# Routed experts on one NeuronCore: gate rows formed on chip instead of gathered, expert rows gathered seven tiles ahead

## What is computed

```
mod = silu(c) @ wmod                      # per batch: sa, ca, ga, sb, cb, gb, 512 each
x   = x + ga * attention(layernorm(x) * (1 + ca) + sa)
h   = layernorm(x) * (1 + cb) + sb
idx = top_k(sigmoid(h @ gate_w.T) + router_bias, 2)          # 2 of 8 experts for each token
w   = chosen scores / their sum
x   = x + gb * (sum over the 2 experts of w * W2[e](silu(h W1[e]) * (h W3[e])) + shared expert(h))
```

## Time and profile before

| | |
|---|---|
| median of 3 runs | 1270.96 us (1268.59 to 1273.08) |
| the profiled execution | 1276.45 us |
| its span, first to last instruction | 1274.7 us |
| PE / DVE / ACT / POOL busy | 95% / 52% / 29% / 43% |
| mean granted clock | 0.987 |
| DMA queues' packet time: q1 (SP's and ACT's among them) / q0 (POOL's) | 40.0% / 26.3% |

### The profile page before, as it was taken

How to read it: one execution, slowest core, us unless ns; L and a number is a source line. 1 busy time by engine, 2 the same in 40 slices (tenths; PEclk the granted TensorE clock), 3 DMA queues, 4 the chain that set the end, 5 groups by cost and what they waited for, 6 DMA issues and landing times.

```text
span 1274.7 us, 25045 instructions
## 1 busy us (share of the span) xinstructions
PE 1209.9 (95%) x9054; PEld 778.4 (61%) x9054; DVE 660.1 (52%) x1357; ACT 372.8 (29%) x802; POOL 545.9 (43%) x479
## 2 busy tenths in 40 slices
PE   7999999999998999999999999899999988999986
PEld 2646666666666666667767767465555555656543
DVE  5557778778765777476765534132223222223312
ACT  4334444444433333333333423011111111111111
POOL 2214556656554444301211102355565555555553
PEclk9999999999999999999999999899999999999988
DMA  7915798998797886453543533679798899898794
GB/s 228 234 44 154 168 220 203 224 228 197 196 197 199 214 221 167 101 131 91 113 129 91 136 80 69 133 153 180 155 177 166 153 164 149 176 179 176 160 159 77
DMA packets 258787, 203.60 MB, mean 160 GB/s; under 512 B 187616, under 2 KB 199904, under 8 KB 258668
## 3 DMA queue, kind: packets, MB, share of 16 engines
q1 hardware_dynamic: 217224, 114.14, 40.0%
q0 software_dynamic: 26192, 64.24, 26.3%
q10 hardware_dynamic: 15256, 23.62, 6.4%
HBM read 104.63 MB, written 53.53 MB: 124 GB/s over the span
## 4 chain that ended last, share of the span: by engine, by line
PE 34%; DMA 30%; issue 14%; POOL 12%; DVE 7%; ACT 2%; SPq 0%; POOLq 0%; ACTq 0%; DVEq 0%
DMA out<-y,slot_row 24%; PE ps_vs L86 3%; PE ps_vs L88 3%; PE ps_vs L87 3%; PE ps_vh L86 2%; POOL h L342 2%; PE ps_vh L88 2%; PE ps_vh L87 2%; PE ps_kh L86 2%; PE ps_kh L88 2%; PE ps_kh L87 2%; POOL xg L350 2%; POOL ol L355 2%; DMA xt<-g 2%; PE ps_qh L86 2%
## 5 line engine op out<-in xcount | busy, mean ns | idle before, releaser
L86 PE MATMUL ps_o<-w_all,xt 128*128 x568 | 181.1, 319 | 31.8 <-DMA xt<-g 31.6
L438 POOL DMA_INDIRECT out<-y,slot_row x71 | 114.4, 1611 | 164.7 <-DMA out<-y,slot_row 122.1
L88 PE MATMUL ps_o<-w_all,xt 128*128 x568 | 180.8, 318 | 0.0
L87 PE MATMUL ps_o<-w_all,xt 128*128 x568 | 180.8, 318 | 0.0
L369 POOL DMA_INDIRECT out<-s_sum,row_no x32 | 53.6, 1675 | 237.6 <-DVE s_sum L622 232.1
L856 DVE SCALAR_TENSOR_TENSOR a<-ps_o,a 128x352 f32<-128x352 f32 x71 | 37.3, 525 | 219.9 <-PE ps_o L88 219.9
L1109 ACT ACTIVATE at<-ps_y 128x384 f16<-128x384 f32 x71 | 34.9, 491 | 264.0 <-PE ps_y L1319 264.0
L868 DVE SCALAR_TENSOR_TENSOR y<-ps_vs,slot_weight,gbr 128x512 f32<-128x512 f32 x71 | 53.3, 751 | 102.5 <-PE ps_vs L88 94.0
L331 POOL TENSOR_TENSOR h<-cen,rows_f 128x512 f32<-128x512 f32 x32 | 40.6, 1270 | 130.0 <-ACT cen L886 113.5
L86 PEld LDWEIGHTS ps_o<-w_all,xt 128*128 128x128 f16 x568 | 56.4, 99 | 64.8 <-issue 37.4
L86 PE MATMUL ps_qh<-ht,wqkv 128*128 128x128 f16 x512 | 87.4, 219 | 1.6 <-DVE wqkv L590 1.6
(11 more groups left out here) (244 smaller groups left out, 3325.4 us busy)
## 6 DMA issues: line engine op xcount, KB each, us to landing
w_stage<-in_w_d ACTq DMA_DIRECT2D x64, 176.0 KB, 2.7
xb<-in_x SPq DMA_DIRECT2D x32, 256.0 KB, 3.3
xr<-in_x SPq DMA_DIRECT2D x32, 256.0 KB, 3.7
out<-x SPq DMA_DIRECT2D x32, 256.0 KB, 3.6
h_d<-hl SPq DMA_DIRECT2D x32, 256.0 KB, 2.5
h2t_d<-h2t SPq DMA_DIRECT2D x32, 256.0 KB, 3.7
s_ht<-h2t_d SPq DMA_DIRECT2D x32, 256.0 KB, 3.6
sstage<-in_sh_flat SPq DMA_DIRECT2D x32, 136.0 KB, 3.2
```

The source lines that it names most:

```text
L86: nc.tensor.matmul(out, lh, rh, start=first, stop=False, skip_group_check=True)
L87: nc.tensor.matmul(out, lh, rl, start=False, stop=False, skip_group_check=True)
L88: return nc.tensor.matmul(out, ll, rh, start=False, stop=last, skip_group_check=True)
L438: pool.indirect_dma_start(m.out, bass.IndirectOffsetOnAxis(ap=m.slot_row[:, t:t + 1], axis=0), m.y[:, t % Y_RING, :], None, compute_op=ALU ...
```

## The change

- `gb_rows_d`, its stores, `slot_batch`, `gbr` and `gather_gate` are gone. `list_tokens` makes instead `batch_weight[b]`, for each slot its weight where its batch is b and 0 elsewhere (one copy and four operations of 128x71 more).
- SP loads the four gate rows, broadcast to 128 partitions, into `gate_rows`, 256 KB each, behind the transposes of tiles 0 to 3.
- Each tile's gate row is a sum of four products: ACT makes the first (`first_gate_row`, an activation with a scale from each partition), DVE adds three (`gate_rows_of`), all 128x512 fp32 in SBUF. `e_out` is now one product of PSUM and this row.
- `G_RING` is 6, so `gather(t + 7)` stands behind `scatter(t)`. The new buffers lie over the shared expert's, so gathers 2 to 6 all wait for `up_done` of the last step, and `e_high(0)` for the shared expert's last add.
- Gathers 0 and 1 now stand ahead of `add_shared(14)`.

```diff
-G_RING, GB_RING, Y_RING = 4, 3, 3
+G_RING, GW_RING, Y_RING = 6, 2, 3
@@ SP
-            for b in range(2):
-                sp.dma_start(rows_of(m.gb_rows_d, b), m.s_gb[:, b, :]).then_inc(m.gb_rows_stored, 16)
...
+    for t in range(4):
+        turn_g(t)
+    sp.wait_ge(m.up_done, EARLY_STEPS)
+    for b in range(B):
+        sp.dma_start(m.gate_rows[:, b, :], m.mod_d[b, 5 * C:6 * C].partition_broadcast(P)).then_inc(m.gates_loaded, 16)
+    for t in range(4, SLOT_TILES):
         turn_g(t)
@@ POOL
-    for q in range(TAIL_STEPS, EARLY_STEPS):
+    for q in range(TAIL_STEPS, EARLY_STEPS - SH_TILES):
         if add_due(q):
             add_shared(q // SH_TILES - 1)
     pool.wait_ge(m.listed, 1)
     pool.wait_ge(m.w_lo, E * WP)
     gather(0)
     gather(1)
-    pool.wait_ge(m.s_t1_done, 3 * BT)
-    pool.wait_ge(m.gb_rows_stored, 16 * B)
-    gather_gate(0)
-    pool.wait_ge(m.at_lo, EARLY_STEPS)
-    gather(2)
-    gather(3)
-    gather_gate(1)
-    gather_gate(2)
-    gather(4)
+    add_shared(CHUNKS - 2)
+    pool.wait_ge(m.up_done, EARLY_STEPS)
+    for t in range(2, G_RING + 1):
+        gather(t)
     add_shared(CHUNKS - 1)
...
     for t in range(SLOT_TILES):
         scatter(t)
         gather(t + G_RING + 1)
-        gather_gate(t + GB_RING)
@@ DVE
+    def gate_rows_of(t, b):
+        v.wait_ge(m.gate_first if b == 1 else m.gate_sum, t + 1 if b == 1 else (B - 1) * t + b - 1)
+        row = m.gate_row[t % GW_RING][:, :]
+        v.scalar_tensor_tensor(out=row, in0=m.gate_rows[:, b, :], scalar=m.batch_weight[:, b, t:t + 1], in1=row,
+                               op0=ALU.mult, op1=ALU.add).then_inc(m.gate_sum, 1)
+
     def e_out(t):
...
-        v.scalar_tensor_tensor(out=m.y[:, t % Y_RING, :], in0=m.ps_ey[:, 0:C], scalar=m.slot_weight[:, t:t + 1], in1=m.gbr[r][:, :],
-                               op0=ALU.mult, op1=ALU.mult).then_inc(m.ey_ready, 1)
+        v.tensor_tensor(m.y[:, t % Y_RING, :], m.ps_ey[:, 0:C], m.gate_row[t % GW_RING][:, :], ALU.mult).then_inc(m.ey_ready, 1)
...
-    for t in range(1, SLOT_TILES):
+    for t in range(1, SLOT_TILES + 1):
         e_low(t - 1)
-        e_multiply(t)
+        gate_rows_of(t - 1, 1)
+        gate_rows_of(t - 1, 2)
+        if t < SLOT_TILES:
+            e_multiply(t)
+        gate_rows_of(t - 1, 3)
         e_out(t - 1)
@@ ACT
+        if t == 0:
+            act.wait_ge(m.s_t1_done, 2 * CHUNKS)          # in e_high
...
+    def first_gate_row(t):
+        at_least(act, m.ey_ready, t - GW_RING + 1)
+        if t == 0:
+            act.wait_ge(m.gates_loaded, 16 * B)
+        act.activation(m.gate_row[t % GW_RING][:, :], m.gate_rows[:, 0, :], ACT.Copy, scale=m.batch_weight[:, 0, t:t + 1]).then_inc(m.gate_first, 1)
+
     e_silu(0)
+    first_gate_row(0)
     for t in range(1, SLOT_TILES):
         e_high(t - 1)
+        first_gate_row(t)
         e_silu(t)
```

More of the change, by code:

```diff
@@ L299, in turn_g @@
     def turn_g(t):
[L300 to L309, removed]
+        if t == 2:
+            sp.wait_ge(m.up_done, EARLY_STEPS - SH_TILES)
+        if t == 4:
+            sp.wait_ge(m.up_done, EARLY_STEPS)
+        sp.wait_ge(m.gathered[t % G_RING], ring_use(t, G_RING))
+        at_least(sp, m.h3_done, t - G_RING + 1)
+        sp.dma_start_transpose(m.xt[t % G_RING][:, :, :], m.g[t % G_RING][:, :]).then_inc(m.xt_loaded[t % G_RING], 16)
+    for t in range(4):
+        turn_g(t)
+    sp.wait_ge(m.up_done, EARLY_STEPS)
+    for b in range(B):
+        sp.dma_start(m.gate_rows[:, b, :], m.mod_d[b, 5 * C:6 * C].partition_broadcast(P)).then_inc(m.gates_loaded, 16)
+    for t in range(4, SLOT_TILES):
         turn_g(t)
@@ L816, in list_tokens @@
         step(v.tensor_copy(m.slot_token[:, :], m.tokenf[:, :]))
-        step(v.tensor_scalar(m.slot_batch[:, :], m.slot_token[:, :], (N // P).bit_length() - 1, None, ALU.logical_shift_right))
+        step(v.tensor_scalar(m.batch_i[:, :], m.slot_token[:, :], N.bit_length() - 1, None, ALU.logical_shift_right))
+        step(v.tensor_copy(m.batchf[:, :], m.batch_i[:, :]))
         step(v.tensor_tensor(m.weightf[:, :], m.listing[:, :, 1], m.listing[:, :, 2], ALU.add))
         step(v.tensor_scalar(m.slot_weight[:, :], m.weightf[:, :], 1.0 / SCALE ** 2, None, ALU.mult))
+        for b in range(B):
+            step(v.scalar_tensor_tensor(out=m.batch_weight[:, b, :], in0=m.batchf[:, :], scalar=float(b), in1=m.slot_weight[:, :],
+                                        op0=ALU.is_equal, op1=ALU.mult))
         step(v.tensor_scalar(m.weightf[:, :], m.weightf[:, :], 0.0, None, ALU.is_le))
@@ L861, in e_low @@
         v.tensor_tensor(m.at[:, t % 2, 1, :, :], m.ps_a[:, :, :], m.at[:, t % 2, 0, :, :], ALU.subtract).then_inc(m.e_at_lo, 1)
+    def gate_rows_of(t, b):
[3 more added lines that the diff above has]
+                               op0=ALU.mult, op1=ALU.add).then_inc(m.gate_sum, 1)
     def e_out(t):
-        r = t % GB_RING
         v.wait_ge(m.ey_done, t + 1)
-        v.wait_ge(m.gbr_loaded[r], ring_use(t, GB_RING))
+        v.wait_ge(m.gate_sum, (B - 1) * (t + 1))
         at_least(v, m.scattered, 16 * (t - Y_RING + 1))
-        v.scalar_tensor_tensor(out=m.y[:, t % Y_RING, :], in0=m.ps_ey[:, 0:C], scalar=m.slot_weight[:, t:t + 1], in1=m.gbr[r][:, :],
-                               op0=ALU.mult, op1=ALU.mult).then_inc(m.ey_ready, 1)
+        v.tensor_tensor(m.y[:, t % Y_RING, :], m.ps_ey[:, 0:C], m.gate_row[t % GW_RING][:, :], ALU.mult).then_inc(m.ey_ready, 1)
     e_multiply(0)
     add(CHUNKS - 1)
-    for t in range(1, SLOT_TILES):
+    for t in range(1, SLOT_TILES + 1):
         e_low(t - 1)
-        e_multiply(t)
+        gate_rows_of(t - 1, 1)
[3 more added lines that the diff above has]
+        gate_rows_of(t - 1, 3)
         e_out(t - 1)
-    e_low(SLOT_TILES - 1)
-    e_out(SLOT_TILES - 1)
 def scalar_program(nc, m, act):
@@ L1366, in place_buffers @@
     END = nc.sbuf_usable_end
-    KEPT = FIRST + 5792
+    KEPT = FIRST + 6400
     SHARED_AT = KEPT + 2 * SH_COLS * 2
@@ L1382, in place_buffers @@
     m.spare_row = sb("spare_row", [P, 1], F32)
-    m.slot_weight = sb("slot_weight", [P, SLOT_TILES], F32)
+    m.batch_weight = sb("batch_weight", [P, B, SLOT_TILES], F32)
     m.eid = sb("eid", [1, SLOT_TILES], I32)
@@ L1492, in place_buffers @@
     m.rowf = sb("rowf", [P, SLOT_TILES], F32)
+    m.slot_weight = sb("slot_weight", [P, SLOT_TILES], F32)
+    m.batch_i = sb("batch_i", [P, SLOT_TILES], I32)
+    m.batchf = sb("batchf", [P, SLOT_TILES], F32)
     sb = region(NAMES_AT + 2 * TILES * E * 4, W_END)
@@ L1495, in place_buffers @@
     m.passed = sb("passed", [1, SLOT_TILES, E], F32)
[L1496 to L1500, removed]
+    GATE_AT, ACT_AT, AT_AT, UP_BYTES = SHARED_AT + 8192, SHARED_AT + 12288, SHARED_AT + 14336, UP_COLS * 2
+    staged, third, second = region(W_STAGE_AT, W_AT), region(SHARED_AT, SHARED_AT + 4096), region(SHARED_AT + 4096, SHARED_AT + 8192)
+    high, low = region(KEPT, KEPT + UP_BYTES), region(KEPT + SH_COLS * 2, KEPT + SH_COLS * 2 + UP_BYTES)
+    m.g = [(staged, staged, second, second, high, high)[j](f"g{j}", [P, 2 * C], F16) for j in range(G_RING)]
+    m.xt = [(staged, staged, third, third, high, high)[j](f"xt{j}", [P, 2 * KC, P], F16) for j in range(G_RING)]
+    m.gate_rows = low("gate_rows", [P, B, C], F32)
+    m.gate_row = [(high, low)[j](f"gate_row{j}", [P, C], F32) for j in range(GW_RING)]
     m.y = region(AT_AT, AT_AT + 6144)("y", [P, Y_RING, C], F32)
@@ L1503, in place_buffers @@
     m.a = sb("a", [P, 2, IT * P], F32)
-    m.at = sb("at", [P, 2, 2, IT, P], F16)
+    m.at = region(GATE_AT, ACT_AT)("at", [P, 2, 2, IT, P], F16)
 def name_semaphores(m, sem):
@@ L1538, in name_semaphores @@
     m.w_loaded, m.w_hi, m.w_lo = ring("w_loaded", W_RING), sem("w_hi"), sem("w_lo")
-    m.gathered, m.xt_loaded, m.gbr_loaded = ring("gathered", G_RING), ring("xt_loaded", G_RING), ring("gbr_loaded", GB_RING)
+    m.gathered, m.xt_loaded = ring("gathered", G_RING), ring("xt_loaded", G_RING)
+    m.gates_loaded, m.gate_first, m.gate_sum = sem("gates_loaded"), sem("gate_first"), sem("gate_sum")
     m.scattered, m.spare_stored = sem("scattered"), sem("spare_stored")
-    m.gb_rows_stored = sem("gb_rows_stored")
     m.h1_done, m.h3_done, m.e_silu, m.e_act = sem("h1_done"), sem("h3_done"), sem("e_silu"), sem("e_act")
@@ L1555, in adaln_block @@
     m.h2_d, m.h2t_d = dram("h2_d", (T, 2 * C), F16), dram("h2t_d", (TILES, P, 2 * C), F16)
-    m.mod_d, m.gab_d, m.gb_rows_d = dram("mod_d", (B, 6 * C), F32), dram("gab_d", (B, C), F32), dram("gb_rows_d", (B * P, C), F32)
+    m.mod_d, m.gab_d = dram("mod_d", (B, 6 * C), F32), dram("gab_d", (B, C), F32)
     with ExitStack() as ctx:
```

8 lines of the change are left out of this document (removed).

## The result

| | before | after |
|---|---|---|
| median (10 runs each, 3 of before from the table above) | 1270.08 us (1261.98 to 1279.01) | 1264.90 us (1260.69 to 1267.02) |
| ratio, 95% interval | | 0.9939 [0.9915, 0.9963] |
| profiled execution / span | 1276.45 / 1274.7 us | 1265.33 / 1263.6 us |
| first and last expert scatter start | 822.6 / 1266.8 | 815.6 / 1255.6 |

1264.9 lies outside the range of 1226 to 1260. The change is faster, but the 24 us of the expert loop didn't come. Of the two profiled spans' difference, 11.1 us, 7.0 come before the first scatter and 4.2 from the loop. These are one execution each, and the one of before lies 6.4 us above its kernel's median. The medians differ by 5.2, less than the start alone brings, so the loop's gain may be nothing.

A forecast was written before the change was run, and what follows sets the result against it. The prediction took the chain of expert scatter landings, 6.35 us a tile, to bound the kernel. From the median of 1270.96 us it took 30.2 (24.2 for the loop, 6.0 for the start), giving 1241; range 1226 to 1260.

The forecast's parts named there:

- What bounds the kernel: Expert loop: each scatter waits for the last one's landing, 6.35 us a tile; PE's 25.8 us of `xt` waits only reflect this.
- Gate gathers gone: Expert loop: DMA share 0.87 to 0.67, landings quicker, period 6.35 to 6.0 us a tile, 24.2 us off.
- Rival B: Expert loop: scatter chain stays slow, transposes may fall on the scatter's packets; period 6.15 to 6.35, 1251 to 1265 us; chance 0.2.
- two laws of load: Scatter landing's excess falls in proportion to load (period 6.15) or as waiting behind a busy server (5.88); 6.0 taken.
- Seven ahead, six buffers: Expert loop: two tiles more lead, 11.7 us, end PE's `xt` waits; `y`'s ring is late next; costed at nothing.
- Gate rows on DVE and ACT: Expert loop: three DVE operations of 0.745 us and ACT's 0.62 a tile lie in waits; no cost.
- The small routing operations: Routing: five more small DVE operations, each under 0.745 us; taken as nothing, bound 3 us.
- The start: Before the expert loop: earlier gathers end PE's wait and half clock; first scatter 816.4 for 822.6, gain 6 us (3.5 to 8.5).
- The path that gave my 816.4: First expert tile: gate rows land at 811, then ACT, DVE and `e_down` lead to the first scatter at 816.4 us.
- The shared port: Expert loop: DVE operations with two SBUF inputs delay POOL's scatter by 0.1 to 0.2 us each, within the 6.0 period.
- rival C: Expert loop: POOL blocked 1.25 us at each scatter by DVE's gate rows; period 7.25, 1328 us; chance 0.06.
- Rival A: Expert loop: PE becomes the bound, period 5.86 us a tile, 34 us off, 1231 us; chance 0.2.

The follow-up runs named there:

- Experiment 8: Kernel before with six buffers and gathers seven ahead, gate gathers kept: 1274.92 us, 1.003.
- 1: Kernel after, transpose of tile t + 7 held until POOL has issued the next scatter and the gather behind it: 1235.4 us, 0.9692.
- 2: Kernel after, transpose of tile t + 7 held until scatter t + 1 has landed: 1234.61 us, 0.969.
- 5: Kernel after, transpose held until scatter t + 1 has landed, then delayed by three small DMAs on SP: 1264.47 us, 0.9963.
- 11: Kernel after with four buffers for six, transpose held until the scatter's landing: 1234.57 us, 0.9684.
- 4: Kernel after without the gate rows of tiles 2 to 70 on ACT and DVE: 1261.44 us, one run.
- experiment 6: Kernel before, only the transpose of tile t + 5 held until scatter t + 1 has landed: 1249.38 us, 0.9856.

## Why the prediction was wrong

**What bounds the kernel: right.** The chain of scatters, the gathers behind it, and PE's waits as their image. Experiment 8 shows the last: with the waits for `xt` gone the time is the same.

**The step that failed: "Gate gathers gone", by which a landing's excess follows the load.** It put the excess of 0.67 us to DMA engines busy 0.87, took 30% to 70% of it off and a period of 6.0 with it. Load fell as reckoned, 0.87 to 0.67, and the period by 0.06. The excess left is in the main one transfer, the transpose, in front of the scatter's packets: with the bytes kept and the order turned it is gone (experiments 1, 2), and with the order turned back it is there again (5). In the sum the term of 24.2 measured 4.2 in the profiled pair, and about nothing by the medians. Load had its part, some 17 us by the estimate above; what the step left out is that taking the gate gathers away also moved the transposes, so that more of them met a scatter. Rival B named the mechanism ("may fall just on the scatter's packets") and had 0.2; the range ended at 1260 inside it. I gave the mean of two laws of load the weight that belonged to an order that the code fixes: gather behind scatter, transpose at the gather's landing. With the gate gathers gone that order got tighter: in the kernel before the middle half of the transposes was issued 0.8 to 2.2 us after a scatter's start (median 1.4), in the kernel after 0.3 to 1.4 (median 0.6), and hits went from 29 to 50 of 70. The median landing rose while the long ones went.

**Seven ahead, six buffers: right,** nothing by itself (8, and 11 against 2). What came late next was not `y`'s ring, as I had said for the lead alone, but the gate row (171.1 us in experiment 8); `y`'s ring it was in the whole change. That PE could "use the chain's quick stretches" gave nothing either, since its lead was used up: DVE's 102.1 us of waiting for landings.

**Gate rows on DVE and ACT: right in effect.** A row took 0.743 to 0.746 us (0.745 forecast), the product 0.69 (0.68); ACT's row 0.72 for 0.62. In the loop they lay in waits (4). The small routing operations cost nothing that shows: PE is busy for all of 700 to 710 us, as before.

**The start: right in size, partly by luck.** First scatter 7.0 us earlier (6.0), no stretch at half clock. The chain of waits of the kernel after shows the loads behind SP's transposes, and then the first expert tile's way:

```profile
802.89 5.21 DMA gate_rows<-mod_d
808.15 0.60 issue
808.75 0.48 ACT at L1105
809.26 0.57 DVE at L849
```

Gate rows came at 808.1 and not 811: I had given the 1 MB of loads beside the gathers too much time. So `y` of tile 0 was ready at 813.2, and `add_shared(15)` was the later condition. Its last add went out at 807.33 and landed at 814.75, where I had 813.3: it was issued 9.4 us earlier than before, but took 7.4 to land for 5.0. The path that gave my 816.4 wasn't the one that ended last, and two misses in opposite directions left 815.6.

**The shared port: right in kind, small here.** Scatters on POOL take 1.57 us in the median of the kernel after, and 1.81 and 1.78 in experiments 1 and 2, where some 60 of 71 scatters start while DVE makes gate rows (9 in the kernel after); the others take 1.57 there too. Experiment 2's DVE and POOL:

```profile
1001.24 1.53 DVE L856 SCALAR_TENSOR_TENSOR gate_row<-gate_rows,batch_weight,gate_row 128x512 f32<-128x512 f32 x2
```

The pair ends at 1002.77; the scatter started at 1002.38 and took 1.83, 0.26 more than 1.57. So rival C's phases did lock in these two, but the price is 0.26 in this scatter and not 1.25, and the period stays at PE's pace. This bears out the rule of the Trainium skill ("SBUF — State Buffer", Who interferes with whom) that a DVE instruction with two SBUF inputs contends with a GpSimd instruction that reads SBUF, here with POOL as the one that comes second.

**Rival A** (PE bound, 1231) is what experiments 1, 2 and 11 reached: 5.84 to 5.88 a tile and 1235.

## What to carry to other kernels

Where a serial chain of transfers sets the pace, ask what stands in front of each link and what starts it, before asking how full the engines are. A transfer that is started by the landing of another, which itself stands behind the link, comes back at the next link with a fixed phase; one wait on the link's own landing moves it out of the way, and it is the first thing to try, since it costs no memory and no engine. To take bytes off pays after that. In the loop it gave at most 4.2 us on the old order (444.2 to 440.0), and 8.8 on the good one (416.8 in experiment 6 to 408.0 in experiment 2). The two medians lie 15 us apart (1249.4 and 1234.6), but the rest of that is the early start, which needs no bytes taken off. And a transfer that is taken away moves the ones that are left: look again at what now meets what.

## What was not expected of the hardware

- Two transfers on different queues didn't share the engines evenly here: the one whose packets came first nearly filled them (q1 85.6% and 92.1% with nothing of q0 beside it, q0 85.5% to 116.9% with 9.0% of q1 or less), and a scatter issued 0.05 us before a transpose still came after it.
- A transpose's packets began 1.2 us after its issue where the engines were free (median of the kernel after and of experiment 2), a scatter's 2.2 after its start. Issue order and order of service differ by that.
- PE's stage ran at 5.84 us a tile in experiment 1, for the 5.86 of one tile before; with 394.00 of 394 us busy (experiment 2) it is the bound.
